# Third attention: its prologue by pairs of token tiles, with the gathered expert rows summed on TensorE

## The reference, cut to what matters

```
# layer 1, feed-forward: 32 experts, top 4, rows computed by seat
eo = (silu(g) * u) @ w2                              # rows of the experts
routed = zeros.at[tok].add(eo[seat] * weight)        # each token: four rows, weighted
x = x + tanh(g_ffn[1]) * (residual + routed + shared)

# layer 2, attention: 32 heads of 8 channels, keys and values from the context
q = layernorm(x) @ Wq.T
q = q * rsqrt(mean(q*q over the head's 8 channels) + 1e-6)      # k likewise
attn = softmax(q @ k.T / sqrt(8))
x = x + tanh(g_xattn[2]) * attn @ v
# then layer 2's feed-forward (8 experts, "golden" router) and layer 3
```

## Time and profile before

| | |
|---|---|
| three runs | 1119.51, 1119.14, 1110.92 us, median 1119.14 |
| profiled execution | 1111.26 us, its span 1109.4 us |
| PE, PEld | 861.1 us (78% of the span), 533.3 us |
| DVE, ACT, POOL | 647.6 us (58%), 517.5 us (47%), 352.2 us (32%) |
| granted TensorE clock, mean | 0.87 of full |
| chain that ended last, by engine | PE 38%, issue 28%, POOL 13%, DVE 9%, ACT 6%, DMA 5% |

### The profile page before, as it was taken

The page is one execution under the profiler, slowest core; times in us unless marked ns, Lnnn a source line. Parts: engine busy times, 40 slices in busy tenths (PEclk is TensorE's granted clock), DMA queues, the critical chain, the costliest instruction groups (busy, mean ns, idle before and its releaser), DMA issues.

```text
span 1109.4 us, 16907 instructions
## 1 busy us (share of the span) xinstructions
PE 861.1 (78%) x6232; PEld 533.3 (48%) x6232; DVE 647.6 (58%) x1315; ACT 517.5 (47%) x884; POOL 352.2 (32%) x304
## 2 busy tenths in 40 slices
PE   4785689995504887225799888977889899999997
PEld 2334446554303666213456444545545555555554
DVE  4968634448742777345424556854767665754443
ACT  2554533442203888213537844356345777533332
POOL 3977123331372000371013575210135432400000
PEclk9776599998656999755758999998989999999999
DMA  9422044421024888330002345211045544533332
GB/s 330 163 71 69 1 123 130 131 84 42 10 100 144 285 286 282 126 92 15 1 1 84 117 130 170 83 46 30 30 136 167 154 124 139 171 109 100 101 100 81
DMA packets 56797, 126.42 MB, mean 114 GB/s; under 512 B 6921, under 2 KB 18569, under 8 KB 56722
## 3 DMA queue, kind: packets, MB, share of 16 engines
q1 hardware_dynamic: 45442, 108.65, 31.5%
q0 software_dynamic: 3072, 8.39, 2.4%
q10 hardware_dynamic: 8208, 8.39, 2.1%
HBM read 82.90 MB, written 42.50 MB: 113 GB/s over the span
## 4 chain that ended last, share of the span: by engine, by line
PE 38%; issue 28%; POOL 13%; DVE 9%; ACT 6%; DMA 5%; SPq 1%; POOLq 0%; DVEq 0%; ACTq 0%
PE ps L1382 12%; PE ps L1325 6%; PE ps L1398 5%; POOL W L710 3%; PE ps L1337 3%; DMA arena<-seats 3%; PE ps L1672 2%; PE ps L1661 2%; PE ps L1686 1%; PE ps L1471 1%; PE ps L1456 1%; POOL wb L713 1%; POOL W L713 1%; POOL k_st L614 1%; POOL k_st L609 1%
## 5 line engine op out<-in xcount | busy, mean ns | idle before, releaser
L1382 PE MATMUL ps<-turned_buf,wb 128*128 128x512 f16 x576 | 138.5, 392 | 10.1 <-POOL wb L713 8.5
L1382 PE MATMUL ps<-turned_buf,W 128*128 128x512 f16 x576 | 135.0, 384 | 6.7 <-POOL W L713 3.3
L2078 DVE SCALAR_TENSOR_TENSOR ctx_sb<-ps,ctx_sb 128x512 f32<-128x512 f32 x96 | 66.3, 691 | 117.3 <-PE ps L1382 75.9
L981 ACT ACTIVATE ctxT<-ctx_sb 128x512 f16<-128x512 f32 x96 | 60.2, 628 | 119.9 <-DVE ctx_sb L2078 119.9
L2085 DVE TENSOR_TENSOR ctxT<-ctx_sb,ctxT 128x512 f16<-128x512 f32 x96 | 68.3, 711 | 68.8 <-ACT ctxT L981 68.4
L710 POOL TENSOR_SCALAR W<-W 128x768 f32<-128x768 f32 x32 | 69.6, 2174 | 120.4 <-ACT wb L993 67.1
L973 ACT ACTIVATE ctx_sb<-ps 128x512 f32<-128x512 f32 x96 | 57.2, 596 | 85.9 <-PE ps L1382 85.7
L1382 PEld LDWEIGHTS ps<-turned_buf,wb 128*128 128x128 f16 x576 | 56.4, 101 | 75.5 <-POOL wb L713 10.0
L1325 PE MATMUL ps<-turned_buf,W 128*128 128x512 f16 x360 | 87.9, 399 | 2.4 <-issue 2.4
L1382 PEld LDWEIGHTS ps<-turned_buf,W 128*128 128x128 f16 x576 | 55.3, 99 | 70.2 <-POOL W L713 5.4
L569 POOL TENSOR_TENSOR rstd<-veps,mhalf 128x4 f32<-128x4 f32 x16 | 18.2, 1139 | 196.1 <-DVE veps L1884 195.2
(11 more groups left out here) (369 smaller groups left out, 1736.5 us busy)
## 6 DMA issues: line engine op xcount, KB each, us to landing
W<-in_w SPq DMA_DIRECT2D x79, 384.0 KB, 3.7
kept<-W SPq DMA_DIRECT2D x24, 384.0 KB, 4.2
kept<-wb SPq DMA_DIRECT2D x24, 384.0 KB, 4.2
W<-kept SPq DMA_DIRECT2D x24, 384.0 KB, 3.0
wb<-kept SPq DMA_DIRECT2D x24, 384.0 KB, 3.0
seats<-wq ACTq DMA_DIRECT2D x1, 8192.0 KB, 37.1
arena<-seats SPq DMA_DIRECT2D x32, 256.0 KB, 3.9
served<-arena SPq DMA_DIRECT2D x32, 256.0 KB, 2.6
```

The costliest lines, as they stand in the source:

```text
L981: nc.scalar.activation(h_16[:, g % 2, 0, :], h_g[:, g % 2, :], ACT.Copy).then_inc(sem("h_hi"), 1)
L1382: last = nc.tensor.matmul(bank(4 + n), w4[k % 4][:, w, n * D + c * P:n * D + (c + 1) * P], x16[:, i, c, half * HALF:(half + 1) * HALF], st ...
L2078: nc.vector.scalar_tensor_tensor(h_g[:, g % 2, :], bank(5), 1.0 / WSCALE, h_s[:, g % 2, :], ALU.mult, ALU.mult).then_inc(sem("gated"), 1)
```

## The change

Nothing of the result is changed. The prologue goes by pairs of tiles, p = 0 to 3. POOL makes 32 diagonal matrices of the weights while the experts run, and PE sums the four gathered rows of a tile as four products with them (`sum_back`); DVE adds the pair's sum to x. `inv_sqrt_pair` stands among POOL's gathers. ACT's Ln and Exp go; DVE starts from an integer guess and takes three Newton steps. Only pair 0 and the sum of pair 1 stand ahead of the units; the rest is laid among them. PE gets products of the identity with itself, whose result nobody reads (`keep_busy`): 12 ahead of the units and one in each unit below 50. ACT takes over every other `o2T`. Further on, POOL's root stands behind the split in step 19, the golden router's weights are made in two pieces with a step between (`golden_fallback`), and DVE makes the low half of one query tile in four in the fourth attention. Cut to its core (lines dedented by eight, "..." where lines are left out):

```diff
@@ -559,11 +575,17 @@
+    def inv_sqrt_pair(p):
+        pool.wait_ge(sem("ln_var"), 2 * 4 + p + 1)
+        nc.gpsimd.tensor_tensor(rstd[:, 2 * p:2 * p + 2], veps[:, 2 * p:2 * p + 2], mhalf[:, 2 * p:2 * p + 2], ALU.pow)\
+            .then_inc(sem("ln_rstd"), 1)
...
@@ -687,7 +709,12 @@
-    pool.wait_ge(sem("seat"), 3)
+    pool.wait_ge(sem("seat"), 4)
+    pool.wait_ge(sem("a1_pv"), 2)
+    for t in range(B):
+        for i in range(TOP1):
+            ins = nc.gpsimd.tensor_scalar(diag(t, i), ident[:, :], m_w[:, t, i:i + 1], None, ALU.mult)
+    ins.then_inc(sem("back_diag"), 1)
@@ -698,9 +725,10 @@
-        if t == 4:
-            inv_sqrt(4, halves=(0,))
-    inv_sqrt(4, halves=(1,))
+            if i == 1 and t in (2, 5):
+                inv_sqrt_pair(t // 2 - 1 if t == 2 else 1)
+    inv_sqrt_pair(2)
+    inv_sqrt_pair(3)
@@ -743,9 +772,9 @@
+        half_step(0, st)
-        half_step(0, st)
@@ -1088,33 +1116,23 @@
+    def q2_x(p):
+        act.wait_ge(sem("turn"), 2 * 4 + p + 1)
+        nc.scalar.activation(xT[:, :, 2 * p * S:2 * (p + 1) * S], bank(5).rearrange("p (c t) -> p c t", c=KD), ACT.Copy)\
+            .then_inc(sem("turned"), 1)
+    def q2_square(p):
+        act.wait_ge(sem("q2_mm"), p + 1)
+        nc.scalar.activation(a2_q[:, 2 * p:2 * p + 2, :, :].rearrange("p b h d -> p (b h d)"), bank(6), ACT.Square)\
+            .then_inc(sem("q2_sq"), 1)
+    def q2_hi(b):
+        act.wait_ge(sem("q2_step"), b // 2 * 4 + b % 2 + 1)
+        nc.scalar.activation(a2_st[:, b, :, 0:2, :], a2_q[:, b, :, :].unsqueeze(2).to_broadcast((P, H2, 2, DH2)),
+                             ACT.Copy).then_inc(sem("q2_hi"), 1)
@@ -1127,14 +1145,17 @@
-        act.wait_ge(sem("o_turn"), m // 2 - 1)
+        if m:
+            act.wait_ge(sem("oT"), m)
+        if m >= 4:
+            act.wait_ge(sem("o_turn"), m // 2 - 1)
...
+    q2_hi(1)
-        if n == 12:
-            q2_x(1)
-        if n == 16:
-            q2_square(1)
-        if n == 19:
-            q2_guess(1)
-        if n == 23:
-            q2_hi(1)
+        if n in (2, 13, 24):
+            q2_x((n + 9) // 11)
+        if n in (4, 15, 26):
+            q2_square((n + 7) // 11)
+        if n in (8, 19, 30):
+            q2_hi((n + 3) // 11 * 2)
+        if n in (9, 20, 31):
+            q2_hi((n + 2) // 11 * 2 + 1)
@@ -1175,7 +1196,7 @@
-        if n >= 37 and n % 4 == 1:
+        if n >= 5 and n % 4 == 1 and oT_by_act(n // 4 - 1):
@@ -1614,31 +1635,50 @@
...
+    def keep_busy(n, k):
+        for i in range(n):
+            nc.tensor.matmul(bank(k), ident16[:, :], ident16[:, :].unsqueeze(1).to_broadcast((P, 4, P)),
+                             start=True, stop=True, skip_group_check=True)
+    def sum_back(p):
+        if p:
+            pe.wait_ge(sem("back_added"), p)
+        else:
+            pe.wait_ge(sem("back_diag"), 1)
+        for t in (2 * p, 2 * p + 1):
+            pe.wait_ge(sem("back", t % 2), 16 * TOP1 * (t // 2 + 1))
+            for i in range(TOP1):
+                last = nc.tensor.matmul(ps[:, 4, (t % 2) * D:(t % 2 + 1) * D], diag(t, i), e_back[:, t % 2, i, :],
+                                        start=(i == 0), stop=(i == TOP1 - 1))
+            last.then_inc(sem("back_read"), 1)
+    def turn_x(p):
+        if p:
+            pe.wait_ge(sem("turned"), 2 * KD * 4 + p)
+        for t in (2 * p, 2 * p + 1):
...
+                k = c * 2 * S + (t % 2) * S
+                last = nc.tensor.transpose(ps[:, 5, k:k + S], xn[:, t, c * P:(c + 1) * P], ident[:, :])
...
+    def queries(p):
+        pe.wait_ge(sem("turned"), 2 * KD * 4 + p + 1)
+        if p:
+            pe.wait_ge(sem("q2_step"), 4 * p)
+        for t in (2 * p, 2 * p + 1):
...
@@ -1697,15 +1737,20 @@
+    sum_back(0)
+    sum_back(1)
+    keep_busy(12, 7)
-        if n == 10:
-            turn_x(1)
-        if n == 14:
-            queries(1)
+        if n in (8, 18):
+            sum_back(n // 8 + 1)
+        if n in (2, 13, 24):
+            turn_x((n + 9) // 11)
+        if n in (3, 14, 25):
+            queries((n + 8) // 11)
@@ -1714,8 +1759,10 @@
-        if n % 8 == 1 and b + 1 < B:
+        if n % 8 == 3 and b + 1 < B:
+        if n < FIRST_UNIT:
+            keep_busy(1, 7)
...
@@ -2289,20 +2340,31 @@
-    def add_back(t):
-        dve.wait_ge(sem("back", t % 2), 16 * TOP1 * (t // 2 + 1))
-        for i in range(TOP1):
-            ins = nc.vector.scalar_tensor_tensor(x[:, t, :], e_back[:, t % 2, i, :], m_w[:, t, i:i + 1], x[:, t, :],
-                                                 ALU.mult, ALU.add)
-            if i < TOP1 - 1:
-                link(ins)
-        ins.then_inc(sem("back_read"), 1)
...
+    def add_back(p):
+        dve.wait_ge(sem("back_read"), 2 * p + 2)
+        both = x[:, 2 * p:2 * p + 2, :].rearrange("p t d -> p (t d)")
+        nc.vector.tensor_tensor(both, bank(4), both, ALU.add).then_inc(sem("back_added"), 1)
+        dve.wait_ge(sem("back_added"), p + 1)
+        for t in (2 * p, 2 * p + 1):
+            ins = nc.vector.bn_stats(stats[:, t, :], x[:, t, :])
+        link(ins)
+        for t in (2 * p, 2 * p + 1):
+            ins = nc.vector.bn_aggr(mv[:, t, :], stats[:, t, :])
+        link(ins)
+        nc.vector.tensor_scalar(veps[:, 2 * p:2 * p + 2], mv[:, 2 * p:2 * p + 2, 1], LN_EPS, None, ALU.add)\
+            .then_inc(sem("ln_var"), 1)
+    def normalise_pair(p):
+        dve.wait_ge(sem("ln_rstd"), 2 * 4 + p + 1)
+        for t in (2 * p, 2 * p + 1):
+            nc.vector.tensor_scalar(xn[:, t, :], x[:, t, :], mv[:, t, 0:1], rstd[:, t:t + 1],
+                                    ALU.subtract, ALU.mult).then_inc(sem("xn_ready"), 1)
...
+    def q2_norm(p):
+        sl = slice(p * per, (p + 1) * per)
+        ms, guess, t = (a2_n[:, i, sl] for i in range(3))
+        dve.wait_ge(sem("q2_sq"), p + 1)
+        link(nc.vector.tensor_reduce(ms, groups[:, sl, :], AX.X, ALU.add))
+        link(nc.vector.tensor_scalar(ms, ms, 1.0 / DH2, RMS_EPS, ALU.mult, ALU.add))
+        link(nc.vector.tensor_scalar(guess.bitcast(I32), ms.bitcast(I32), -0.5, ROOT_BITS, ALU.mult, ALU.add))
+        for k in range(3):
+            link(nc.vector.tensor_tensor(t, guess, guess, ALU.mult))
+            link(nc.vector.tensor_tensor(t, t, ms, ALU.mult))
+            link(nc.vector.tensor_scalar(t, t, -0.5, 1.5, ALU.mult, ALU.add))
+            link(nc.vector.tensor_tensor(guess, t, guess, ALU.mult))
+    def q2_scale(p):
+        for b in (2 * p, 2 * p + 1):
...
+    def q2_lo(b):
+        dve.wait_ge(sem("q2_step"), b // 2 * 4 + 2)
+        dve.wait_ge(sem("q2_hi"), b + 1)
+        nc.vector.tensor_tensor(a2_st[:, b, :, 2:4, :], a2_q[:, b, :, :].unsqueeze(2).to_broadcast((P, H2, 2, DH2)),
+                                a2_st[:, b, :, 0:2, :], ALU.subtract).then_inc(sem("q2_step"), 1)
@@ -2366,14 +2430,13 @@
-    for t in range(4):
-        add_back(t)
-    statistics(4, 0)
-    add_back(4)
-    normalise(4, 0)
-    add_back(5)
-    q2_squares(0)
+    add_back(0)
+    normalise_pair(0)
+    q2_scale(0)
+    q2_lo(0)
+    q2_lo(1)
+    add_back(1)
+    def golden_fallback(h):
+        ...                      # the second half of golden_weights, called one step later

@@ -2432,22 +2499,24 @@
-        if n in (2, 4):
-            add_back(5 + n // 2)
-        if n == 5:
-            statistics(4, 1)
-        if n == 8:
-            normalise(4, 1)
-        if n == 18:
-            q2_squares(1)
-        if n == 22:
-            q2_norm(1)
+        if n in (0, 12, 23):
+            normalise_pair((n + 10) // 11 + (n == 0))
+        if n in (6, 17, 28):
+            q2_norm((n + 5) // 11)
+        if n in (7, 18, 29):
+            q2_scale((n + 4) // 11)
+        if n in (9, 20, 31):
+            q2_lo((n + 2) // 11 * 2)
+        if n in (10, 21, 32):
+            q2_lo((n + 1) // 11 * 2 + 1)
+        if n in (11, 21):
+            add_back((n + 9) // 10)
-        if n % 8 == 1 and n // 8 + 1 < B:
+        if n % 8 == 4 and n // 8 + 1 < B:
-        if 5 <= n < 37 and n % 4 == 1:
-            o2T((n - 5) // 4)
+        if n >= 5 and n % 4 == 1 and n < 37 and not oT_by_act(n // 4 - 1):
+            o2T(n // 4 - 1)
@@ -2502,6 +2575,13 @@
+    def q3_lo(b):
+        dve.wait_ge(sem("q3_hi"), b + 1)
+        nc.vector.tensor_tensor(a3_st[:, b % 4, :, 2:4, :],
+                                a3_y[:, b, :].rearrange("p (h d) -> p h d", d=DH3).unsqueeze(2).to_broadcast((P, H3, 2, DH3)),
+                                a3_st[:, b % 4, :, 0:2, :], ALU.subtract).then_inc(sem("q3_lo"), 1)
@@ -2581,6 +2661,8 @@
+            if s == 13:
+                q3_lo(4 * h)
```

More of the change, by code:

```diff
@@ L30 @@
 U8 = mybir.dt.uint8
+I32 = mybir.dt.int32
 ACT = mybir.ActivationFunctionType
@@ L70 @@
 ROUND = 1.5 * 2.0 ** 23
+ROOT_BITS = float(0x5f3759df)
 def build(nc, a, out):
@@ L295, in build @@
         h_16 = ctxT[:, :, :, :].rearrange("p c b s -> p (c b s)")[:, 0:T].bitcast(F16).rearrange("p (k i t) -> p k i t", k=2, i=2)
+        diags = [v.rearrange("p (t i q) -> p t i q", i=TOP1, q=P) for v in
```

(47 more changed lines are left out.)

52 lines of the change are left out of this document (4 added, 48 removed).

## The result

The changed kernel takes **1126.69 us**, median of 20 runs (1114.83 to 1133.49), against 1115.87 for 20 runs of the kernel before (1110.92 to 1121.97) on the same chips: ratio 1.0076, interval 1.0055 to 1.0097; two of the 20, over 1.5% above the fastest, are left out of the ratio. The forecast was 1098, from 1082 to 1116. The sum had been 18 us less; by the ratio it is 8.5 more. The profiled execution took 1122.22 us.

A forecast was written before the change was run, and what follows sets the result against it. Bounds: a chain of small steps ahead of the units, PE at half clock in them. Terms -16 + 5 - 5.5 - 1.5 = -18 took the profiled 1111.3 to 1093.3; half of 7.9 put back gave 1098 us, range 1082 to 1116.

The forecast's parts named there:

- Diagonals on POOL, 0: During the experts: POOL's 32 diagonal weight instructions, 19 us, are hidden and slow no exposed DVE work; cost 0.
- Ahead of the units, -16: First gather to first scores: first scores start at 493.3 instead of 509.3, 16 us less (bounds -14.5 and -18).
- Units 0 to 50, +5: Stretch of units up to 50: 92.3 us against 87.3, so 5 us more.
- Filler 0.22 us: In each unit to 50: one filler product on PE adds 0.22 us at the higher clock.
- The clock stays up but for unit 12: Units 0 to 50: priced at the higher clock, 81.9 us, with one fall in unit 12's wait costing 3.6.
- Newton waits, 1.5 for all: Units 6, 17 and 28: waits from DVE's Newton chains, `q2T(4)` late by about 1; 1.5 us for all.
- Twelve stalls at the copy, 7.9: Units 0 to 50: twelve stalls at the copy of the sums, 0.66 us each after the filler's cover, 7.9.
- Unit 12, 5.3: Unit 12: PE waits 5.3 us because pair 2's root stands on POOL behind the gathers of tiles 6 and 7.
- half-way rival: Units 0 to 50: clock holds to unit 26, then drops at `turn_o2`; 9 us more, 1107; chance 0.25.
- Golden weights, -1.5: Golden router: making its weights in two pieces removes PE's wait for DVE, 1.5 us less (bounds 0 and -3).
- Step 19, -5.5: Third feed-forward network: POOL's split ahead of the root saves 3.0 of wait and 2.5 of clock, 5.5 us less.
- q3_lo, 0: Making a quarter of q3_lo on DVE instead of POOL changes nothing: 0 (bounds -1 and +2).

The follow-up runs named there:

- experiments 1 to 4: Changed kernel without unit fillers (0.9975); with `turn_q2` and `q2T` placed earlier again (0.9959); with both (0.9872); with golden weights in one piece (1.0024).
- run 9: The kernel of run 5 without the 12 fillers ahead of the units: 1098.86 us, 0.9851.
- run 2: Changed kernel with `turn_q2` and `q2T` back at each eight's second unit from unit 17, and q2T(2) ahead of the normalising in unit 12: 1113.99 us, 0.9959.
- run 10: Changed kernel with three fillers instead of one in each of units 25 to 49, one execution only: 1123.98 us.
- run 4: Changed kernel with the golden router's weights in one piece again: 1121.1 us, 1.0024.
- run 3: Changed kernel without fillers in the units and with the edits of run 2: 1103.31 us, 0.9872.
- run 5: Changed kernel without fillers in the units, with the edits of run 2 and golden weights in one piece: 1098.08 us, 0.9838.

## Why the prediction was wrong, step by step

**Diagonals on POOL, 0:** held, as far as the runs can tell. POOL hid them. The first gather came 1.9 later than before, but it starts between 457.75 and 460.04 in the runs of experiments 1 to 4 with the same diagonals, and at 458.87 and 460.0 in the two kernels without them.

**Ahead of the units, -16:** right. First scores were at 492.56 where 493.3 was forecast; counted from the first gather it is -18.7, just past the bound of -18. Step by step: root of pair 0 done at 476.6 (475.5), last gather of tile 3 issued 484.4 and used at 486.31 (485), turning at 490.73. The fillers stood in the shadow of the scaling instead of on the path (run 9). One reading was wrong: the 0.325 us for each query record "at the lower clock" is a mean over both levels, for in the kernel before the clock was at 0.50 until 494.1 and at 1.00 behind it. The sum for one pair of queries, 2.6, lies between the 1.99 and 3.78 measured above.

**Units 0 to 50, +5: this is the step that failed**; it measured +24.8. The forecast total was 92.3, the measured one 112.1. Its terms:
- *Filler 0.22 us.* I took one of twelve in a row. Between products of other shapes it costs 0.32, at the lower clock 0.53: 50 x 0.1 = 5.
- *The clock stays up but for unit 12.* This is the larger part. It fell at `turn_o2(2)`, and PE did 18 more units at 1.62 instead of 0.99, three `turn_o2` at up to 3.63 instead of 1.98, with turnings: 11 + 4 + 2 = 17. The fall in unit 2, at 494.9, cost 3 more (1.8 of it on the queries). That in unit 12, priced at 3.6, cost 4.5: 0.9.
- *Newton waits, 1.5 for all.* In unit 28 alone it was 2.15, where I had `q2T(4)` late "by about 1": 0.7 more. The clock fell right behind it, but in run 2 it fell at the same place without the wait.
- *Twelve stalls at the copy, 7.9.* Here the fillers covered nearly all; idle time other than in units 12 and 28 is 8.8 - 4.1 - 2.2 = 2.5. That is 5.4 in favour.
- *Unit 12, 5.3:* PE was idle for 4.1, at the right place (0.3 + 1.0 + 1.0 + 1.8), 1.2 in favour. The mechanism was right: the root behind the gathers ends last, and in run 10 it holds up PE by itself, for 5.99. What I hadn't foreseen is the standstill beside it: PE's small products were drawn out in the time in which PE would have waited anyway.

These come to 5 + 17 + 3 + 0.9 + 0.7 - 5.4 - 1.2 = 20.0, against 19.8.

The half-way rival (chance 0.25) had almost the place: the clock holds while sums and queries are dense, and drops at a `turn_o2`. Run 2 bears it out most plainly. Why the clock falls there no run took apart. It was priced as down for half of the three tiles, 9 us; the clock stayed down for all of them, with a dearer filler. Whoever reads 35.1 of 36.8 us busy at 0.50 in the earlier trace rows has the evidence that a busy PE doesn't bring the clock back by being busy. I used it against the rival and then let a small filler do it.

**The rule weighed there.** After the change the clock fell in or right behind idle time of PE in units 2, 12, 28, 52 and 54. The Trainium skill (TensorE: Matmul & The Clock Gate, "HAM oscillation") says that idle gaps bring the clock down; the profile of the changed kernel agrees, though the waits of the page's example are longer than most of these. Other traces don't: the clock also fell at 556.89 in run 2, 546.25 in run 10 and 544.37 in run 4, with PE idle for 0.27 us at most in the 8 us before, each time 2.2 to 2.6 us behind the start of a `turn_o2`. Nor do the units run at full clock without fillers: run 3, which has neither them nor the waits of units 28 and 52, has 0.66. And 41.95 us without a gap didn't bring the clock back. What makes it fall without idle time is open.

**The total.** The sum gave 1093.3; with half of the 7.9 put back that is 1097.3, and not 1098 as written. It makes no difference here.

**After unit 50, not in the forecast: +7.1.** Two steps I costed at nothing. `q2T(7)`, moved by three units, came behind DVE's golden distances: PE waited 1.67, the clock fell behind it, and the `turn_o2` behind it took 3.60 instead of the 1.98 of the earlier trace rows. *Golden weights, -1.5* had the wrong sign: the second piece stands in front of the instruction that frees PE's bank, and PE waited 3.86. Run 4 puts it at 6 us and run 5 at 4, neither clear of noise; the wait itself is gone in run 4. A part of this is that two of its steps grew from 0.16 to 0.83 and from 0.25 to 1.49 beside POOL's split. The Trainium skill (SBUF — State Buffer, "SBUF: two separate sides") says that a DVE instruction with two inputs in SBUF is locked out while POOL's reads; the growth agrees with it, and no run took it apart.

**Step 19, -5.5:** PE's first wait went from 4.52 to 1.58, and its clock stayed up (2.76 for the 12 products instead of 5.30), as forecast: -5.5. But the next split was late by the root, 1.36 us. By the stretch it gave 3.3; alone, on the kernel before, -0.1% (-0.3 to +0.1).

**q3_lo, 0:** nothing measurable; the rest of the span differs by 0.8.

## What to carry to other kernels

A filler on PE must be priced among its neighbours, not in a row with its like, and at both clocks; even one that holds the clock can cost more than the clock gives. When a step is moved later on an engine, write down which instruction stands ahead of it there in each period: the two places in run 2 held waits of 3.8 us together, and the edit that took them away gave some 13 us in all. Where a wait seems to explain a fall of the clock, take the wait away and see whether the fall stays. If a rival's mechanism has your own rows behind it, price it at its full length.
